# An attention layer on one core: the first loads and the last tile are arranged anew

## The reference

```
q, k, v = x @ Wq.T + bq, x @ Wk.T + bk, x @ Wv.T + bv      # x is 4096 x 128, fp32
scores = where(adj > 0, q @ k.T / sqrt(128), -9e15)        # adj is 4096 x 4096, int32
att = softmax(scores) @ v
y = x + elu(att)
out = (y - mean(y)) / sqrt(var(y) + 1e-5)                  # over the 128 columns of a row
```

## Time and profile before

| | |
|---|---|
| median of 3 runs | 458.83 us (458.31 to 459.29) |
| the profiled execution: its own time | 457.99 us |
| its span, first to last instruction | 456.2 us |
| PE busy | 437.3 us, 96% |
| DVE, ACT, POOL busy | 374.4, 356.7, 277.9 us |
| mean granted clock of TensorE | 0.993 |

### The profile page before, as it was taken

How to read it: one execution, slowest core, us unless ns; L and a number is a source line. 1 busy time by engine, 2 the same in 40 slices (tenths; PEclk the granted TensorE clock), 3 DMA queues, 4 the chain that set the end, 5 groups by cost and what they waited for, 6 DMA issues and landing times.

```text
span 456.2 us, 11774 instructions
## 1 busy us (share of the span) xinstructions
PE 437.3 (96%) x3587; PEld 324.2 (71%) x3587; DVE 374.4 (82%) x656; ACT 356.7 (78%) x650; POOL 277.9 (61%) x436
## 2 busy tenths in 40 slices
PE   5998999999999999999999999999999999999982
PEld 3564677777777777777777777777777777777761
DVE  0768888999889888898898988899898988889630
ACT  3768777777887888777787887877788787877882
POOL 0065246667766666667766666667766666666675
PEclk9999999999999999999999999999999999999997
DMA  8834999999999999999999899999999999994440
GB/s 232 343 111 141 237 251 225 189 249 246 232 219 250 230 236 241 203 242 222 231 230 240 236 231 241 226 215 241 222 234 225 245 236 233 241 217 89 76 70 17
DMA packets 128428, 96.90 MB, mean 212 GB/s; under 512 B 103328, under 2 KB 112032, under 8 KB 128416
## 3 DMA queue, kind: packets, MB, share of 16 engines
q1 hardware_dynamic: 127984, 96.68, 88.6%
q10 hardware_dynamic: 432, 0.07, 0.1%
HBM read 69.47 MB, written 2.10 MB: 157 GB/s over the span
## 4 chain that ended last, share of the span: by engine, by line
PE 91%; ACT 3%; DVE 2%; DMA 1%; issue 1%; POOL 1%; SPq 0%; POOLq 0%; ACTq 0%; DVEq 0%
PE ps_out L656 24%; PE ps_t L633 15%; PE ps_out L658 12%; PE ps_scores L619 12%; PE ps_scores L618 12%; PE ps_scores L617 12%; PE ps_t L564 2%; PE ps_out L575 2%; DMA x_rows<-in_x_dram 1%; PE ps_out L564 1%; DVE scores L501 1%; ACT scores L389 1%; DVE p_lo L516 1%; PE ps_scores L585 1%; ACT p_hi L398 1%
## 5 line engine op out<-in xcount | busy, mean ns | idle before, releaser
L501 DVE CUSTOM_DVE_ANT_0 scores<-ps_scores,adj 128x1024 f32<-128x1024 f32 x128 | 155.8, 1217 | 1.8 <-issue 0.5
L516 DVE TENSOR_TENSOR p_lo<-ps_t,p_hi 128x512 f16<-128x512 f32 x160 | 108.6, 688 | 49.3 <-ACT p_hi L398 44.2
L398 ACT ACTIVATE p_hi<-ps_t 128x512 f16<-128x512 f32 x160 | 94.8, 593 | 68.5 <-PE ps_t L633 66.3
L389 ACT ACTIVATE scores<-scores,neg_max 128x1024 f32<-128x1024 f32 x128 | 145.8, 1139 | 0.1
L656 PE MATMUL ps_out<-v_parts,p_hi 128*128 128x257 f16 x640 | 124.8, 274 | 0.9 <-DVE p_lo L516 0.8
L658 PE MATMUL ps_out<-v_parts,p_lo 128*128 128x129 f16 x640 | 116.1, 218 | 0.0
L280 POOL TENSOR_TENSOR p_rows<-scores,p_rows 128x1024 f16<-128x1024 f32 x64 | 106.1, 1659 | 11.2 <-ACT p_rows L406 11.2
L487 DVE TENSOR_SCALAR adj<-adj 128x1024 f32<-128x1024 int32 x128 | 108.7, 849 | 0.0
L633 PEld LDWEIGHTS ps_t<-ident,scores 128*128 128x128 f32 x640 | 79.2, 141 | 34.2 <-ACT scores L389 5.2
L633 PE MATMUL ps_t<-ident,scores 128*128 128x128 f32 x640 | 96.4, 273 | 3.2 <-ACT scores L389 3.2
L617 PE MATMUL ps_scores<-k_hi,q_hi 128*128 128x512 f16 x256 | 96.7, 378 | 0.5 <-DVE max_parts L501 0.5
(11 more groups left out here) (56 smaller groups left out, 404.0 us busy)
## 6 DMA issues: line engine op xcount, KB each, us to landing
adj<-in_adj_dram SPq DMA_DIRECT2D x128, 512.0 KB, 4.9
x_rows<-in_x_dram SPq DMA_DIRECT2D x4, 512.0 KB, 6.0
out_dram<-y_out SPq DMA_DIRECT2D x32, 64.0 KB, 4.6
p_turned<-p_rows SPq DMA_TRANSPOSE x64, 5.2
w_rows<-in_L_gnn_Wk_dram SPq DMA_DIRECT2D x1, 64.0 KB, 4.3
bv_rows<-in_L_gnn_bv_dram ACTq DMA_DIRECT2D x1, 64.0 KB, 4.4
w_rows<-in_L_gnn_Wq_dram SPq DMA_DIRECT2D x1, 64.0 KB, 4.0
w_rows<-in_L_gnn_Wv_dram SPq DMA_DIRECT2D x1, 64.0 KB, 4.3
```

What stands on the lines that cost most here:

```text
L389: nc.scalar.activation(s_sb[s][:, cols], s_sb[s][:, cols], ACT.Exp, bias=neg_max[:, s:s + 1]).then_inc(exp_done, 1)
L398: nc.scalar.activation(p_hi[:, k, :], ps_t[bank_of(s, g)][:, :], ACT.Copy).then_inc(phi_ready, 1)
L501: nc.vector.tensor_tensor_reduce(out=s_sb[s][:, cols], in0=ps_scores[c % 2][:, :], in1=mask_sb[s][:, cols], scale=SCALE, scalar=-3.0e38, o ...
L516: nc.vector.tensor_tensor(p_lo[:, k, :], ps_t[bank_of(s, g)][:, :], p_hi[:, k, :], ALU.subtract).then_inc(plo_ready, 1)
```

## The change

x comes in five chunks instead of four: 4, 4, 8, 8 and 8 tiles (256, 256, 512, 512, 512 KB). The three weight loads go from SP's queue to ACT's. The bias columns go to SP's queue between the second chunk of x and the third; `bv_rows` goes to SP's queue behind the last chunk and ahead of adj. PE, once the identity is there, runs nine transposes of the identity into `ps_t[1]`, whose result nothing reads. The end of tile 31 no longer runs on ACT and POOL, but on DVE (`finish_last`), with one exponential on ACT and one power on POOL; the mean and variance come from `bn_stats` and `bn_aggr`. SP's last store waits for `last_done`.

```
+LAST_OPS = 10
+WARM_UP = 9
+X_CHUNKS = ((0, 1), (1, 2), (2, 4), (4, 6), (6, 8))
...
         def _(sp):
-            for n in range(4):
+            for n, (begin, end) in enumerate(X_CHUNKS):
+                tiles = slice(begin * BLOCKS, end * BLOCKS)
+                sp.dma_start(x_rows[:, tiles, :], x_tiled[:, tiles, :]).then_inc(x_in[n], 16)
                 if n == 1:
-                    sp.dma_start(w_rows[:, 1, :], wk).then_inc(w_in, 16)
-                    sp.dma_start(w_rows[:, 0, :], wq).then_inc(w_in, 16)
-                    sp.dma_start(w_rows[:, 2, :], wv).then_inc(w_in, 16)
-                sp.dma_start(x_rows[:, n * XQ:(n + 1) * XQ, :], x_tiled[:, n * XQ:(n + 1) * XQ, :]).then_inc(x_in[n], 16)
+                    sp.dma_start(b_cols[:, 0:1], bq.rearrange("(p a) -> p a", a=1)).then_inc(b_in, 16)
+                    sp.dma_start(b_cols[:, 1:2], bk.rearrange("(p a) -> p a", a=1)).then_inc(b_in, 16)
+            sp.dma_start(bv_rows[:, :], bv.rearrange("(a d) -> a d", a=1).to_broadcast([P, D])).then_inc(bv_in, 16)
...
-            for i in range(TILES - 2, TILES):
-                store(i, i % 2)
+            store(TILES - 2, 0)
+            sp.wait_ge(last_done, LAST_OPS)
+            sp.dma_start(out_tiled[TILES - 1], y_out[:, 1, :]).then_inc(stored[1], 16)
...
         def _(pool):
...
-            period(TILES + 2, 0, has_rows=False)
+            pool.wait_ge(last_done, 9)
+            nc.gpsimd.tensor_tensor(rstd[:, 1:2], var_eps[:, 1:2], stat_consts[:, 3:4], ALU.pow).then_inc(last_rstd, 1)
...
         def _(act):
-            act.dma_start(b_cols[:, 0:1], bq.rearrange("(p a) -> p a", a=1)).then_inc(b_in, 16)
-            act.dma_start(b_cols[:, 1:2], bk.rearrange("(p a) -> p a", a=1)).then_inc(b_in, 16)
-            act.dma_start(bv_rows[:, :], bv.rearrange("(a d) -> a d", a=1).to_broadcast([P, D])).then_inc(bv_in, 16)
+            act.dma_start(w_rows[:, 1, :], wk).then_inc(w_in, 16)
+            act.dma_start(w_rows[:, 0, :], wq).then_inc(w_in, 16)
+            act.dma_start(w_rows[:, 2, :], wv).then_inc(w_in, 16)
...
-            period(TILES + 2, 0, has_1=False, has_2=False)
+            act.wait_ge(last_done, 4)
+            nc.scalar.activation(exp_neg[:, 1, :], neg[:, 1, :], ACT.Exp).then_inc(last_exp, 1)
...
         def _(dve):
+            def finish_last(i, s):
+                one = slice(s, s + 1)
+                dve.wait_ge(pv_done, STEPS * (i + 1))
+                nc.vector.reciprocal(recip[:, one], ps_out[s][:, 2 * D:2 * D + 1]).then_inc(last_done, 1)
+                dve.wait_ge(last_done, 1)
+                dve.wait_ge(bv_in, 16)
+                nc.vector.scalar_tensor_tensor(out=att_sum[:, s, :], in0=ps_out[s][:, 0:D], scalar=recip[:, one],
+                                               in1=bv_rows[:, :], op0=ALU.mult, op1=ALU.add).then_inc(last_done, 1)
+                dve.wait_ge(last_done, 2)
+                nc.vector.scalar_tensor_tensor(out=att[:, s, :], in0=ps_out[s][:, D:2 * D], scalar=recip[:, one],
+                                               in1=att_sum[:, s, :], op0=ALU.mult, op1=ALU.add).then_inc(last_done, 1)
+                dve.wait_ge(last_done, 3)
+                nc.vector.tensor_scalar(neg[:, s, :], att[:, s, :], 0.0, None, ALU.min).then_inc(last_done, 1)
+                nc.vector.scalar_tensor_tensor(out=res[:, s, :], in0=att[:, s, :], scalar=0.0, in1=x_rows[:, i, :],
+                                               op0=ALU.max, op1=ALU.add).then_inc(last_done, 1)
+                dve.wait_ge(last_exp, 1)
+                dve.wait_ge(last_done, 5)
+                nc.vector.scalar_tensor_tensor(out=y[:, s, :], in0=exp_neg[:, s, :], scalar=-1.0, in1=res[:, s, :],
+                                               op0=ALU.add, op1=ALU.add).then_inc(last_done, 1)
+                dve.wait_ge(last_done, 6)
+                nc.vector.bn_stats(moment_parts[:, :], y[:, s, :]).then_inc(last_done, 1)
+                dve.wait_ge(last_done, 7)
+                nc.vector.bn_aggr(moments[:, :], moment_parts[:, :]).then_inc(last_done, 1)
+                dve.wait_ge(last_done, 8)
+                nc.vector.tensor_scalar(var_eps[:, one], moments[:, 1:2], EPS, None, ALU.add).then_inc(last_done, 1)
+                dve.wait_ge(last_rstd, 1)
+                dve.wait_ge(stored[s], 16 * (i // 2))
+                nc.vector.tensor_scalar(y_out[:, s, :], y[:, s, :], moments[:, 0:1], rstd[:, one],
+                                        ALU.subtract, ALU.mult).then_inc(last_done, 1)
...
         def _(pe):
...
             pe.wait_ge(ident_set, 1)
+            for n in range(WARM_UP):
+                nc.tensor.transpose(ps_t[1][:, n % BLOCKS * P:(n % BLOCKS + 1) * P], ident[:, :], ident[:, :])
             transpose_x(0)
             transpose_x(1)
```

More of the change, by code:

```diff
@@ L98, in attention_kernel @@
         y_out = sb("y_out", [P, 2, D], F32)
+        moment_parts = sb("moment_parts", [P, 6], F32)
+        moments = sb("moments", [P, 2], F32)
         w_in = sem("w_in")
@@ L103, in attention_kernel @@
         bv_in = sem("bv_in")
-        x_in = [sem(f"x_in{n}") for n in range(4)]
+        x_in = [sem(f"x_in{n}") for n in range(len(X_CHUNKS))]
         consts_set = sem("consts_set")
@@ L140, in attention_kernel @@
         pool_done = sem("pool_done")
+        last_done = sem("last_done")
+        last_exp = sem("last_exp")
+        last_rstd = sem("last_rstd")
         stored = [sem(f"stored{n}") for n in range(2)]
@@ L145, in attention_kernel @@
         out_tiled = out.rearrange("(t p) d -> t p d", p=P)
-        XQ = TILES // 4
         def ps_xt(g):
@@ L521, in reciprocal @@
                 nc.vector.reciprocal(recip[:, s:s + 1], ps_out[s][:, 2 * D:2 * D + 1]).then_inc(recip_ready, 1)
-            def period(p, n, has_scores=True, has_1=True, has_2=True, warm=True, makes_mask=True):
+            def finish_last(i, s):
[27 more added lines that the diff above has]
+                                        ALU.subtract, ALU.mult).then_inc(last_done, 1)
@@ L525, in period @@
+            def period(p, n, has_scores=True, has_1=True, has_2=True, warm=True, makes_mask=True, last=False):
                 for j in range(STEPS):
@@ L533, in period @@
                             low_part(p - 1, 1 - n, g)
-                    if j == 7 and has_2:
+                    if j == 7 and has_2 and not last:
                         reciprocal(p - 2, n)
@@ L555, in _ @@
             period(TILES, 0, has_scores=False)
-            period(TILES + 1, 1, has_scores=False, has_1=False)
+            period(TILES + 1, 1, has_scores=False, has_1=False, last=True)
+            finish_last(TILES - 1, 1)
         @block.tensor
@@ L579, in transpose_x @@
             def transpose_x(g):
-                if g % 2 == 0:
-                    pe.wait_ge(x_in[g // 2], 16)
+                for n, (begin, end) in enumerate(X_CHUNKS):
+                    if g == begin:
+                        pe.wait_ge(x_in[n], 16)
                 if g >= 4:
```

## The result

The changed kernel takes 456.2 us in the median of 10 runs (454.56 to 457.37), the kernel before 458.54 (457.62 to 461.34). The ratio is 0.9941, with a 95% interval of 0.992 to 0.9962. So it is 2.3 us faster by the medians, 2.7 by the ratio. The forecast was 454.8, in a range of 453.6 to 456.4: the time lies inside, but 1.4 us over the point. Of the 4.0 us that the sum promised, 2.3 to 2.7 came.

A forecast was written before the change was run, and what follows sets the result against it. PE was taken to bound the steady periods, which the change leaves alone. The profiled 457.99 - 0.2 (loads) - 0.7 (clock) - 3.1 (end) gave 453.99, and 0.84 more for the median gave 454.8 us, range 453.6 to 456.4.

The forecast's parts named there:

- The end: Last tile's serial chain, moved mostly to VectorE: 3.53 us instead of 6.58, a gain rounded to 3.1 us, bounds 2.3 to 3.4.
- the term with the widest bounds: bn_stats in the last tile's chain: not in the trace, between 0.15 and 0.69 us, taken as 0.29 plus 0.04 handover.
- The loads: At the start: the x chunk with tiles 8 to 15 lands 0.2 us earlier, at 8.0, with bv_rows behind all of x.
- The second rival: At the start: bias columns hold up the third x chunk by up to 1.6 us, time 456.3; chance 0.10.
- The clock: At the start: nine transposes raise PE's clock by 8.0 us; group 2 to 3 takes 2.15 us, not 2.85, gaining 0.70.
- the start: Loads and early clock before the steady periods: 0.2 + 0.7 = 0.9 us gained, carried to the end by PE's chain.
- The first: At the start: PE's clock rises no earlier than before, so the 0.7 us is not gained, time 455.5; chance 0.22.
- The third rival: The start's 0.9 us is absorbed in the VectorE stretch from 39.71 us, time 455.7; chance 0.05.
- The fourth rival: Steady periods get longer as VectorE loses its 1.3 us slack; at 0.2 us a period, 460.4; chance 0.03.

The follow-up runs named there:

- e1: Changed kernel with the old loads and no transposes of the identity, so only the new end against the kernel before: 455.76 us, ratio 0.9931.
- e4: Changed kernel with twelve transposes of the identity first, one between groups 0 and 1, four behind the weights' transposes: 454.67 us, ratio 0.9911.
- e7: Changed kernel with its nine transposes of the identity and four more behind the transposes of the weights: 454.8 us, ratio 0.9917.
- e2: Changed kernel with the old end put back, so only the new start against the kernel before: 458.89 us, ratio 1.0.
- e9: e4's kernel with the old end, where ACT and POOL finish the last tile: 457.75 us, ratio 0.9967.
- e11: The changed kernel unaltered, timed again beside e4's kernel: 456.89 us, ratio 0.9934.
- e8: e4's kernel without the four transposes behind the weights' transposes, leaving the last hole: 455.53 us, ratio 0.9933.
- e5: Changed kernel with the old order of the loads and eighteen transposes of the identity instead of nine: 454.79 us, ratio 0.991.
- e3: Changed kernel without the nine transposes of the identity: 456.33 us, ratio 0.9944.
- e12: e4's kernel unaltered, timed again beside the changed kernel: 454.33 us, ratio 0.9891.

## Why the prediction was right, and where it was not

**The end: right.** 3.53 us were forecast, 3.62 measured, in place of 6.58. `bn_stats`, the term with the widest bounds, took 0.29 us as forecast, `bn_aggr` 0.18, the operations from PSUM 0.35. Only the last operation, a tensor-scalar with two values per partition, took 0.35 us instead of 0.22. e1 gives 3.1 us for the end in executed time.

**The loads: about right in the first profile, not shown as a gain.** The chunk that PE waits for last landed 0.23 us earlier (2.81 + 5.14 = 7.95 against 8.18). But this isn't steady: the group behind it began at 7.89 to 8.67 us in the ten profiles with the new order in which PE waited for it, 8.19 in the mean, and at 8.23, 8.24 and 8.32 in the three with the old one. What holds the chunk up in some executions was not tried, nor whether the bias columns do. The second rival's size is not seen: no group 2 that waited for the chunk began after 8.67, where the rival asked for 9 or more. One reading beside it was off, at no cost: SP's three 512 KB loads of 3.32 us are 1.1 us each, not 0.45, and `bv_rows` took SP 1.54, so that its first load of adj began at 7.80 instead of 6.18 us.

**The clock: the step that failed.** It is "If PE's activity from 1.8 us on counts, with holes of about 1 us, the clock has risen by 8.0 us", worth 0.70 us. The activity does count (e4). The holes were seen but passed over. With them, the clock has risen by 8.0 in a part of the executions (e7's profile, whose start is the same up to there, and by their times the shortest of the changed kernel). In others it rises near 13 us (both profiles of the changed kernel), later than in the kernel before, where PE went from 5.55 to 8.23 us with a hole of only 0.10. e2's profile, with the same start, lies between, with a step of 2.97 us. The price of the late rise is 4.32 - 2.22 = 2.1 us between groups 2 and 3. On the whole the outcomes about cancel: the start as changed is worth 0.0 us (e2, interval ±0.9) instead of 0.9. With the holes filled it is worth 1.2 (e9).

**How far the range was luck.** The 456.2 us lie in the range, whose upper part was put there for a late third chunk (the second rival, 456.3). What took its place was the late clock, and none of the rivals had the clock rise later than before. Timed again (e11), the same kernel had a median of 456.89 us, outside the range, though with nearly the same ratio to the kernel before (0.9934 against 0.9941). The end's 3.1 us were understood; that the rest came out inside was partly luck.

**The rivals.** The first, "the clock rises no earlier", at 455.5, was nearest in mechanism, yet it took the old time of the rise as the worst case. There was a worse one: that the change itself delays it. Its time, by the profiles, is 454.8 + 4.32 - 2.15 = 457.0, where the long executions stand (456.5 to 457.8 in e8 and e11). The rule in "TensorE: Matmul & The Clock Gate" of the Trainium skill, section "Part 4: PE-mode transpose", by which the high clock does not engage for transposes, does not hold for these 128x128 fp32 ones: e4's clock is up after transposes alone.

The third rival (absorbed) is true in part, at another place and by another wait than it named. PE's transposes of the probabilities, in the kernel before and in e4's:

```profile
53.85 0.38 PE L617 MATMUL ps_scores<-k_hi,q_hi 128*128 128x512 f16 x1
54.63 0.66 PE L633 MATMUL ps_t<-ident,scores 128*128 128x128 f32 x4
...
51.45 1.06 ACT L416 ACTIVATE p_rows<-scores 128x1024 f16<-128x1024 f32 x1 [1.92 <-DMA p_turned<-p_rows]
52.93 0.38 PE L668 MATMUL ps_scores<-k_hi,q_hi 128*128 128x512 f16 x1
54.09 0.66 PE L684 MATMUL ps_t<-ident,scores 128*128 128x128 f32 x4 [0.35 <-ACT scores L399]
```

e4's PE is 0.92 us ahead at the scores, as it was when the transposes of group 5 began (12.75 against 13.67). Then it waits 0.35 us for ACT's exponentials, which stand behind ACT's wait for the transposes made by DMA, and is 0.54 us ahead there and 0.55 at the last reciprocal (447.01 against 447.56). So about 60% of that lead reached the end. In e5's profile a second such wait follows, 0.46 us at 96.38 us, and its last reciprocal (447.95) is later than that of the kernel before, though its group 3 began earlier (10.53 against 11.08). How much such waits cost in the medians was not measured. The fourth rival fails: the two periods compared have kept their 12.75 and 12.76 us.

**What stays open.** How large a hole may be, and where it may lie, was not measured. Why the changed kernel had two of seven good executions in e11, and four of ten under 455.6 us in the first measurement, is not told apart from chance. Nor is it explained why the kernel before, with hardly a hole, spreads over 2.4 to 3.7 us in its four sets of executions.

## What to carry to other kernels

Here, work that keeps TensorE busy until the data comes had to reach up to the data. A stretch of it at the beginning with a hole of 0.8 us behind it gave nothing that shows (e3); with four more transposes in that hole none of six executions took over 456 us (e7), where 11 of 17 of the changed kernel did. With the small holes filled too, the spread went from some 3 us to about 1 or less (e4, e12). When a load is cut up so that its first part comes sooner, look for what TensorE then does until the last part; finishing early may only make a hole. And where a chain of small operations stands alone at the end, a price per operation from the trace's own rows, plus the handovers, can give its length closely: 3.53 us against 3.62 here. A lead won at the start has to be followed to the end of the trace: part of it can be lost at a later wait.

## What the runs showed of the hardware

The time at which TensorE's clock rises differs from execution to execution with the same work ahead of it: the step from group 2 to group 3 was 2.85 us in the kernel before and 2.47 in e1, and with the changed start 4.32 (twice: the changed kernel and e11) and 2.97 (e2). About 2 us of the whole time hang on it. One profile of each kernel would have shown the last reciprocal of the changed kernel 1.89 us late, and that would have been taken for fixed. A hole of 1.0 to 1.1 us after the rise did not bring the clock down (e7, e8: group 2 in 0.66 us). A plain fp32 matmul of 128 columns costs twice a transpose of that size (5.49 us for twelve against 2.82, at the low clock for nearly all of it), so the two can't be exchanged one for one as filling.
